# Decoder layer: the second attention weighted with unnormalised exponentials, divided afterwards

## The reference

```python
q = query.reshape(b, sq, h, d)            # h = 16, d = 8, sq = 256
kv = key_value.reshape(b, skv, h, d)      # skv = 64
qh = jnp.einsum('bshd,hed->bshe', q, wq) + bq
kh = jnp.einsum('bthd,hed->bthe', kv, wk) + bk
vh = jnp.einsum('bthd,hed->bthe', kv, wv) + bv
scores = jnp.einsum('bshd,bthd->bhst', qh, kh) / jnp.sqrt(jnp.asarray(d, qh.dtype))
attn = jax.nn.softmax(scores, axis=-1)
ctx = jnp.einsum('bhst,bthd->bshd', attn, vh)
out = ctx.reshape(b, sq, e)
return out @ wo.T + bo
...
x = _layernorm(x + self_attention(x))
x = _layernorm(x + second_attention(x, ctx_1024))
x = _layernorm(x + feed_forward(x))
```

## Time and profile before

| | |
|---|---|
| median of 3 runs | 1008.93 us (1008.55 to 1009.18) |
| the profiled execution: its own time | 1014.34 us |
| the profiled execution: span from first to last instruction | 1012.2 us |
| PE busy | 849.9 us (84%) |
| DVE busy | 802.7 us (79%) |
| ACT busy | 660.7 us (65%) |
| POOL busy | 425.7 us (42%) |
| mean granted TensorE clock | 0.969 |

### The profile page before, as it was taken

The page is one execution under the profiler, slowest core; times in us unless marked ns, Lnnn a source line. Parts: engine busy times, 40 slices in busy tenths (PEclk is TensorE's granted clock), DMA queues, the critical chain, the costliest instruction groups (busy, mean ns, idle before and its releaser), DMA issues.

```text
span 1012.2 us, 18717 instructions
## 1 busy us (share of the span) xinstructions
PE 849.9 (84%) x6181; PEld 663.4 (66%) x6181; DVE 802.7 (79%) x2564; ACT 660.7 (65%) x1938; POOL 425.7 (42%) x356
## 2 busy tenths in 40 slices
PE   6898888888888898888889889888888888888774
PEld 5667666765766676576767657666765766676552
DVE  6665779788888978898897888788787988888545
ACT  4475767757685766767676675767667576766532
POOL 0244162543616253361635346173534617253431
PEclk9799999999999999999999999999999999999795
DMA  6000000000100000000100001000100001000000
GB/s 189 6 1 6 6 27 7 6 12 6 28 12 6 6 13 26 6 6 12 27 6 7 11 6 28 11 6 7 27 11 7 6 12 27 1 6 6 6 1 10
DMA packets 26414, 15.56 MB, mean 15 GB/s; under 512 B 4304, under 2 KB 25552, under 8 KB 26320
## 3 DMA queue, kind: packets, MB, share of 16 engines
q1 hardware_dynamic: 26320, 14.38, 5.0%
HBM read 12.27 MB, written 2.10 MB: 14 GB/s over the span
## 4 chain that ended last, share of the span: by engine, by line
PE 45%; DVE 25%; ACT 18%; issue 6%; POOL 4%; DMA 2%; DVEq 0%; ACTq 0%; POOLq 0%
PE psY L600 12%; ACT pr L1319 9%; PE psS L566 6%; PE psT L586 5%; PE psS L636 4%; ACT sq L1291 3%; POOL pr L1519 3%; PE psJ L441 3%; PE psS L548 3%; PE psJ L443 2%; PE psJ L442 2%; DVE xp L1061 2%; DVE xmax L1059 2%; DVE ssq L957 2%; ACT xpT L1367 2%
## 5 line engine op out<-in xcount | busy, mean ns | idle before, releaser
L1519 POOL TENSOR_TENSOR pr<-pr,rden 128x512 f32<-128x512 f32 x192 | 192.9, 1040 | 379.2 <-ACT pr L1319 195.8
L600 PE MATMUL psY<-val,pT 128*128 128x128 f32 x1536 | 206.5, 281 | 31.3 <-ACT pT L1334 23.7
L1319 ACT ACTIVATE pr<-pr,nmin 128x256 f32<-128x256 f32 (+1 forms) x512 | 225.3, 443 | 10.8 <-DVE nmin L1004 10.2
L600 PEld LDWEIGHTS psY<-val,pT 128*128 128x128 f32 x1536 | 186.6, 193 | 41.8 <-issue 22.2
L1004 DVE CUSTOM_DVE_ANT_0 pr<-psS,alibi,nullmin 128x256 f32<-128x256 f32 (+1 forms) x512 | 183.7, 414 | 26.4 <-PE psS L566 24.4
L1510 POOL TENSOR_TENSOR qk<-qk,rn 128x1024 f32<-128x1024 f32 x64 | 121.1, 1913 | 88.8 <-DVE x L870 50.2
L586 PE MATMUL psT<-ident,pr 128*128 128x128 f32 x768 | 116.9, 279 | 20.2 <-POOL pr L1519 20.2
L566 PE MATMUL psS<-kT,qT 64*128 64x256 f32 (+1 forms) x1024 | 111.7, 346 | 19.3 <-DVE nmin L1004 12.9
L586 PEld LDWEIGHTS psT<-ident,pr 128*128 128x128 f32 x768 | 88.9, 143 | 39.9 <-POOL pr L1519 32.7
L566 PEld LDWEIGHTS psS<-kT,qT 64*128 64x128 f32 x1024 | 78.2, 189 | 48.5 <-DVE nmin L1004 19.4
L1319 ACT ACTIVATION_READ_ACCUMULATOR pr<-pr,nmin 128x1 f32 x512 | 96.6, 189 | 0.0
(11 more groups left out here) (138 smaller groups left out, 1663.5 us busy)
## 6 DMA issues: line engine op xcount, KB each, us to landing
w1s<-w1b SPq DMA_DIRECT2D x8, 258.0 KB, 2.9
xin<-x SPq DMA_DIRECT2D x16, 128.0 KB, 2.1
xres<-x SPq DMA_DIRECT2D x16, 128.0 KB, 2.1
w2s<-w2T SPq DMA_DIRECT2D x8, 256.0 KB, 3.2
out<-x SPq DMA_DIRECT2D x16, 128.0 KB, 1.8
pr<-w_q SPq DMA_DIRECT2D x1, 512.0 KB, 3.8
pr<-w_kv SPq DMA_DIRECT2D x1, 512.0 KB, 5.0
pr<-wvT SPq DMA_DIRECT2D x1, 512.0 KB, 4.5
```

The costliest lines, as they stand in the source:

```text
L600: mm = pe.matmul(psY[t], pT[c % 4][:, P * j:P * (j + 1)], val[:, kt, P * h:P * (h + 1)], start=(blk == 0), stop=False)
L1319: act.activation(pr[t][:, h, :], pr[t][:, h, :], ACT.Exp, bias=nmin[:, t, h:h + 1], scale=-1.0, accum_out=dparts[:, t, h, 0:1]).then_inc(e ...
L1519: pool.tensor_tensor(pr[t][:, hs, :], pr[t][:, hs, :], rden[:, t, hs].unsqueeze(2).broadcast_to([P, heads, P * (t + 1)]), ALU.mult).then_i ...
```

## The change

The exponentials are no longer normalised. PE transposes and weights them as they are, and a second set of eight products per tile, with the mask of ones xwide in the place of the values, gives the sum of a head's exponentials in each of that head's feature rows. The weighted features now stand in psS2 columns 0 to 255 and the sums in columns 256 to 511. DVE takes the reciprocal of the sums (128x256) and multiplies the features by it into xoT (`divide_cross`); it does so behind layer norm 2 and ahead of `ln1_begin`. `cross_denominators`, `norm_cross` and `copy_xoT` go. The bias of v is added to the values once, in iteration 0, on DVE, when they are copied out of psJ (it may be, as the weights of a head sum to one after the division); it is loaded as a 128x128 broadcast.

```diff
@@ SP, loads
-            sp.dma_start(xb[:, 2:3], xbv).then_inc(g_loaded, 16)
+            sp.dma_start(bv[:], xbv.rearrange("d a -> a d").broadcast_to([P, P])).then_inc(g_loaded, 16)
@@ PE
-                    take(f'J{k % 2}', kvx_copied, k + 3)
+                    take(f'J{k % 2}', vx_biased, k + 1)
...
-                pe.wait_ge(xprobs_normed, NT * b + t + 1)
+                pe.wait_ge(xexp_done, NT * b + t + 1)
...
-                for r in range(2):
-                    for j in range(XH // 4):
-                        mm = pe.matmul(psS[2][32 * j:32 * (j + 1), SEQ + P * t:SEQ + P * (t + 1)], vexp[b % 2][:, j, r, :],
-                                       xpT[j // 2][:, P * (2 * (j % 2) + r):P * (2 * (j % 2) + r + 1)],
-                                       start=(r == 0), stop=(r == 1))
+                for what, col in ((vexp[b % 2], P * t), (xwide, SEQ + P * t)):
+                    for r in range(2):
+                        for j in range(XH // 4):
+                            mm = pe.matmul(psS[2][32 * j:32 * (j + 1), col:col + P], what[:, j, r, :],
+                                           xpT[j // 2][:, P * (2 * (j % 2) + r):P * (2 * (j % 2) + r + 1)],
+                                           start=(r == 0), stop=(r == 1))
                 mm.then_inc(xpv_done, 1)
 
             def merge_cross_heads(b):
-                pe.wait_ge(xoT_copied, b + 1)
+                pe.wait_ge(xoT_divided, b + 1)
@@ DVE
-            def cross_denominators(b, t):
-                dve.wait_ge(xexp_done, NT * b + t + 1)
-                steps.mark(dve.tensor_reduce(xden[:, t, :], xp[t][:], AX.X, ALU.add))
-                steps.wait(dve)
-                dve.reciprocal(xrden[:, t, :], xden[:, t, :]).then_inc(xrden_ready, 1)
+            def divide_cross(b):
+
+                dve.wait_ge(xpv_done, NT * (b + 1))
+                steps.mark(dve.reciprocal(xrec[:], psS[2][:, SEQ:2 * SEQ]))
+                steps.wait(dve)
+                dve.tensor_tensor(xoT[:], psS[2][:, 0:SEQ], xrec[:], ALU.mult).then_inc(xoT_divided, 1)
+
+            def bias_context_values():
+
+                for k in range(4):
+                    dve.wait_ge(kvx_ready, k + 3)
+                    dve.tensor_tensor(vx[:, 4 * k:4 * k + 4, :], psJ[k % 2][:].rearrange("p (b d) -> p b d", b=4),
+                                      bv[:].unsqueeze(1).broadcast_to([P, 4, P]), ALU.add).then_inc(vx_biased, 1)
...
+                if not c:
+                    bias_context_values()
                 if a:
                     sum_squares(i + 1, 0, 0)
                 copy_pT(i, 6)
                 if a:
                     sum_squares(i + 1, 0, 1)
                     floor_squares(0)
-                if c:
-                    cross_denominators(i - 1, 0)
                 copy_pT(i, 8)
-                if c:
-                    cross_denominators(i - 1, 1)
...
                 ln2_end(i)
+                if c:
+                    divide_cross(i - 1)
                 if d:
                     ln1_begin(i + 2)
@@ ACT
-            def copy_xoT(b):
-
-                act.wait_ge(xpv_done, NT * (b + 1))
-                act.activation(xoT[:], psS[2][:, SEQ:2 * SEQ], ACT.Identity, bias=xb[:, 2:3]).then_inc(xoT_copied, 1)
@@ POOL
-            def norm_cross(b):
-                for t in range(NT):
-                    pool.wait_ge(xrden_ready, NT * b + t + 1)
-                    pool.tensor_tensor(xp[t][:], xp[t][:], xrden[:, t, :].unsqueeze(2).broadcast_to([P, XH, CTX]),
-                                       ALU.mult).then_inc(xprobs_normed, 1)
```

More of the change, by code:

```diff
@@ L149, in program @@
         xw = sb("xw", [P, 3, P])
-        xb = sb("xb", [P, 3])
+        xb = sb("xb", [P, 2])
         xwo = sb("xwo", [P, P])
@@ L154, in program @@
         vx = sb("vx", [P, NB, P])
+        bv = sb("bv", [P, P])
         w1s = sb("w1s", [P, OC, P + 1])
@@ L198, in program @@
         xoT = sb("xoT", [P, SEQ])
+        xrec = sb("xrec", [P, SEQ])
         xmax = sb("xmax", [P, NT, XH])
         xp = [sb(f"xp{t}", [P, XH, CTX]) for t in range(NT)]
-        xden = sb("xden", [P, NT, XH])
-        xrden = sb("xrden", [P, NT, XH])
         xpT = [sb(f"xpT{k}", [P, 512]) for k in range(2)]
@@ L296, in program @@
         xs_sub = sem("xs_sub")
-        xrden_ready = sem("xrden_ready")
+        xoT_divided = sem("xoT_divided")
+        vx_biased = sem("vx_biased")
         y2_added = sem("y2_added")
@@ L322, in program @@
         xexp_done = sem("xexp_done")
-        xoT_copied = sem("xoT_copied")
         w12raw_copied = sem("w12raw_copied")
@@ L330, in program @@
         probs_normed = sem("probs_normed")
-        xprobs_normed = sem("xprobs_normed")
         kexp_ready = sem("kexp_ready")
@@ L1224, in _ @@
             cross_shift(b, 2)
-            cross_denominators(b, 0)
             cross_shift(b, 3)
             add_h2(b - 1)
-            cross_denominators(b, 1)
+            divide_cross(b)
             ln4_end(b - 1)
@@ L1273, in context_kv @@
                                    bias=xb[:, 1:2]).then_inc(kvx_copied, 1)
[L1274 to L1277, removed]
             def copy_qk(n, c):
@@ L1467, in iteration @@
                 copy_x1T(i)
-                if c:
-                    copy_xoT(i - 1)
                 copy_xqT(i)
@@ L1497, in _ @@
                 copy_xpT(b, k)
-            copy_xoT(b)
             ln_seed("ln3", (0, 1), NB)
@@ L1535, in spread_context @@
                 if isinstance(b, int) and b == 0:
-                    pool.wait_ge(kvx_copied, 6)
+                    pool.wait_ge(kvx_copied, 2)
+                    pool.wait_ge(vx_biased, 4)
                     pool.wait_ge(xwide_ready, 5)
@@ L1567, in iteration @@
                 spread_context(i)
-                if c:
-                    norm_cross(i - 1)
                 if a:
@@ L1579, in _ @@
             x2_plus_bias(NB - 2, GROUPS - 1)
-            norm_cross(NB - 1)
             x2_plus_bias(NB - 1, GROUPS - 1)
```

## The result

The changed kernel takes 1047.3 us (median of 4 runs, 1042.7 to 1049.6) beside 1008.7 of the kernel before: ratio 1.038 (1.033 to 1.042). Six more runs of it gave 1045.7, ratio 1.037 (1.035 to 1.040). The forecast was 1050, with a range from 1034 to 1064. The profiled execution took 1045.0 us, with a span of 1043.2.

A forecast was written before the change was run, and what follows sets the result against it. It took DVE's chain from the second attention's sums to the qT copies as the bound; 7 x 2.2 + 7 x 3.3 = 38.5 us, plus 3.3 at the end, on 1008.9 gave 1050.7, rounded to 1050, range 1034 to 1064.

The forecast's parts named there:

- The split into kinds: Iterations alternate: seven even ones were to grow by 2.2 us each, seven odd ones by 3.3 us.
- Reciprocal 1.65 us: DVE's 128x256 reciprocal from PSUM in the division: 1.65 us, with bounds of 0.42 and 2.79 us.
- 0.58 us per block of products: PE's added psS<-xpT products with the mask: 0.58 us per block of 16 instructions, uncovered; bounds nothing and 1.2.
- Queue behind the division 2.65 us, stalls gone: DVE from division to first qT copy: 2.65 us left of 5.30, as 2.65 of stalls against POOL's qk pass go.
- Some 4 us of idle DVE in front of a queue that was the chain: DVE, ready for the division near 563, waits for PE's products until 566.97, delaying null scores, v and qT copies.
- PE's wait for pT goes, 1.08 us in even iterations: Before the first attention's last products PE stops waiting for DVE's pT copy: 1.08 us earlier in even iterations, 0 in odd.
- PE's path only 0.8 or 1.9 late, hidden behind DVE's: PE's merge comes 0.8 us late in even and 1.9 in odd iterations, less than DVE's qT copies.
- The end, 3.3 us: Last iteration: second products 0.7 late, division near 1003.0 where PE's merge began at 999.69, so 3.3 us more.
- 1050.7 as the median plus 41.8: Whole kernel: 38.5 us for fourteen iterations plus 3.3 at the end, added to the median of 1008.9.
- neither cheap nor steep: Rival reciprocal costs on DVE: 0.42 us gives 1031 (0.13 for all 1031 cases); 2.2 us or more, 1059 and up (0.17).
- PE's path is all that counts: Rival: DVE's queue has unseen slack, only PE's delay remains, 22 us, 1031; the 1031 cases together have 0.13.
- The faster case: Rival: DVE's load bounds, the division fills former stall time if products end before 564.6 (odd: 623.8); 994 us, chance 0.03.

The follow-up runs named there:

- products alone: Kernel before with only the products with the mask of ones added, their result unused: 1022.9 us, ratio 1.014.
- place alone: Changed kernel without the mask's products and with a 128x256 copy instead of the reciprocal: 1009.4 us, ratio 1.000.
- short reciprocal: Changed kernel with a copy of the same 128x256 from PSUM instead of the reciprocal: 1025.6 us, ratio 1.017.
- no products: Changed kernel without the mask's products, the reciprocal taken of the weighted features: 1033.6 us, ratio 1.024.
- the two swaps: Kernel before with DVE's pT copy ahead of the norms: 1009.6 us; the same plus ACT's second xpT copy ahead of the seed: 1008.3 us.
- the four corners: Changed kernel with mask's products and reciprocal (1045.7 us), products and a copy (1025.6), reciprocal without products (1033.6), copy without products (1009.4).

## Why the prediction was right, point by point

The mechanism and the sign were right, and the iterations nearly to the number; the term for the end was not. What a pair grew by:

| | predicted | measured | from |
|---|---|---|---|
| mask's products, four blocks | 2.32 | 1.70 to 1.78 | products alone; place alone against short reciprocal; no products against changed |
| reciprocal beyond a copy's 0.42 | 2.46 | 2.64 to 2.66 | short reciprocal; no products against place alone |
| the rest: place, stalls, PE's wait | 0.72 | 0.74 | place alone |
| sum | 5.5 | 5.16 | changed kernel |

The 0.72 is only what is left of 5.5 when the first two rows are taken off; that it meets the 0.74 is partly chance. The split into kinds was right as well: from one iteration's first copy of qT to the next one's, the stretch grows by 2.0 to 2.2 us where it ends in an even iteration and by 3.1 to 3.5 where it ends in an odd one, and 2.2 and 3.3 were predicted (the first and the last of the fourteen left out).

- *Reciprocal 1.65 us:* 1.758. Through 0.253 us at 16 elements that makes 6.27 ns per element and a fixed part of 0.153, where I took 5.8 and 0.161 (one of the two rows reads from SBUF, the other from PSUM, so this slope is an estimate). The upper bound of 2.79 should have been 2.77. The Trainium skill's repeat count of 8 ("VectorE: DVE Perf Modes", First, the fixed hardware budget) led to 2.25; the trace does not agree.
- *0.58 us per block of products:* mis-sized. The step took the distance from a block to the transposes behind it. The block with the mask starts 0.43 us after the one with the values (575.99 to 576.42); why the step to the transposes is longer was not tested. Of the pair's 5.5 us, this is 0.6 too much.
- *Queue behind the division 2.65 us, stalls gone:* right. The product ends at 583.33, and the first copy of qT starts at 585.91, 2.6 us later. The Trainium skill's "SBUF — State Buffer", Who interferes with whom, is borne out by the rows again: the null scores' add takes 225 ns without POOL's pass beside it, and 1809 ns with it, in iteration 0 at 90.71, where the pass runs from 88.62 to 92.44. That the page's other half spares the new product no run here shows: the pass is over before the product starts in all 16.
- *"Some 4 us of idle DVE in front of a queue that was the chain":* 3.73, so the wait was right, but as a price it was half a reading. Filling it won 0.2 us an iteration, and the place alone costs 0.37 an iteration. The price was in the added products and in the reciprocal, which stand in the path to qT; the idle time came in the place of work and stalls that had gone.
- *PE's wait for pT goes, 1.08 us in even iterations:* the wait went and PE's next wait is 0.50 as before. By itself its loss gains nothing as long as DVE's work stays, as the two swaps show; without the sums and POOL's pass it was worth 7.7 us in the fourteen iterations, where 7 x 1.08 makes 7.6.
- *PE's path only 0.8 or 1.9 late, hidden behind DVE's:* PE's wait at the merge is 0.73 in the even iteration, followed by one of 0.96 at qT. The wait at qT is the later one, as said.
- *The end, 3.3 us:* wrong, and the largest error. The fourteen iterations grew by 35.7 us (38.5 predicted) and the spans by 35.5 like against like, so the end cost nothing. From PE's last scores to its last merge it took 15.36 us before (984.33 to 999.69) and takes 14.08 after (1016.60 to 1030.68):

```profile
1016.60 2.08 PE L635 MATMUL psS<-kexp,xqT 64*128 64x512 f32 x4 [3.27 <-DVE xp L1061]
...
1020.78 1.91 PE L659 MATMUL psT<-ident,xp 128*128 128x128 f32 x8
...
1027.26 0.64 PE L672 MATMUL psS<-xpT,vexp 128*32 128x128 f32 x16 [0.74 <-ACT xpT L1364]
...
1030.68 1.22 PE L680 MATMUL psS<-xwo,xoT 128*128 128x128 f32 x4 [2.34 <-DVE xoT L1069]
```

  The step counted 1.46 us of DVE's work as gone ahead of the exponentials, and put the first products some 0.1 to 0.4 late. It left out that POOL's pass stood in this path too: before, PE had waited 2.55 us for it ahead of the first transposes, and these now follow the scores after 4.18 us instead of 6.94. It also took 1.08 us per block from the earlier trace rows. The granted clock was 0.50 there, and is 0.84 in the window of these products now (1020 to 1030 us); a block takes 0.64. How much of the end is order and how much is clock stays open: without the mask's products the end was not shorter but longer (91.6 us behind the last first copy, beside 89.9), at a granted clock of 0.50 from 1000 us to its end at 1031.
- *1050.7 as the median plus 41.8:* with 35.7 for the iterations and no end it is 1008.9 + 35.7 = 1044.6, beside 1045.7 in the larger set of runs. The 1047.3 of the first four lies between two of 1042.7 and 1045.0 and two of 1049.6, so that 1050 came so close to it is in part luck: the sum was some 6 us too large.
- *Rivals:* the reciprocal is neither cheap nor steep, at 1.758 us. That PE's path is all that counts is refuted by the copy in its place: 20 us less. The faster case needed the products at 564.6, where they ended at 581.1 in a trace that runs some 12 us later at this point; the four corners show products and reciprocal in full on the path.

## What to carry to other kernels

Ask of new work first whether an engine that is already late waits for what it makes; how long an engine idles in front of it says less. Here 4 blocks of products and 2 reciprocals a pair were paid in full, while the new place, with 2.8 us of idle time in an iteration, cost 0.4, since work and stalls had gone. Normalising late makes the division wide: the 16 sums of a token became 128, one for each feature, and the reciprocal went from two of 16 columns, 0.253 us each, to one of 256 columns and 1.758 us at the latest point of the stage. Measure first what the removed work is worth, by leaving it out: 12 us was about the most that this change could have won.

## What the runs showed of the hardware

- A reciprocal of float32 on DVE takes 1.758 us for 128x256 from PSUM, 6.9 ns per column with its fixed part, where a copy of the same takes 0.425 us, 1.7 ns per column. With the 0.253 us for 128x16 from SBUF that makes an estimate of 6.27 ns for each further column. ACT's logarithm and exponential of the same 128x256 take 0.38 and 0.42 us, 0.8 together.
- Sixteen matmul instructions with 32 columns of weights, behind sixteen of the same kind, lengthen the path by 0.43 to 0.44 us, at a granted clock of 1.00 (windows from 560 to 590 us of the changed kernel).
- Executions of one program lie up to 8 us apart (1042.7 to 1050.1 here, 1006.3 to 1014.4 before), the longer ones at a lower mean granted clock, and two profiled ones differ by the granted clock in the first 60 us and by 4.5 us there.
- Taking a wait of 1.08 us from PE by two different swaps left the pair at 117.70 us beside 117.59: PE's chain and DVE's end within about a microsecond of each other.
